# Reordering the last stage of a one-core mixture-of-experts kernel: root chain, last load, stores and last sum

## The reference

```python
x = x + layernorm(attention(layernorm(x)))          # linear attention, 16 heads
x = x + layernorm(ffn(layernorm(x)))
# ffn: out = swiglu(x, shared weights) + sum over the 2 best of 8 experts of w_e * swiglu(x, expert e)
```

## Time and profile before

| what | us |
|---|---|
| three runs | 618.5, 621.85, 625.44 |
| median | 621.85 |
| the profiled execution: device time | 621.5 |
| its span, first to last instruction | 619.8 |
| busy in the span: PE, DVE, ACT, POOL | 456.2, 330.1, 272.4, 270.9 |

### The profile page before, as it was taken

How to read it: one execution, slowest core, us unless ns; L and a number is a source line. 1 busy time by engine, 2 the same in 40 slices (tenths; PEclk the granted TensorE clock), 3 DMA queues, 4 the chain that set the end, 5 groups by cost and what they waited for, 6 DMA issues and landing times.

```text
span 619.8 us, 9478 instructions
## 1 busy us (share of the span) xinstructions
PE 456.2 (74%) x2583; PEld 365.0 (59%) x2592; DVE 330.1 (53%) x1405; ACT 272.4 (44%) x633; POOL 270.9 (44%) x328
## 2 busy tenths in 40 slices
PE   5859888888888983597269963097999987799600
PEld 5637665656565653486258862094689876698600
DVE  6796978787878682155132442032122221795477
ACT  5544655565556551254035620033243544245654
POOL 3000154545454537136745157654026556346620
PEclk9998999999999997599669996589899999799855
DMA  8940010101010103355225442144145557884554
GB/s 254 306 166 2 5 49 32 46 34 45 34 44 34 49 26 125 91 155 158 82 87 158 134 139 66 44 130 153 51 124 167 147 149 221 271 297 147 191 168 192
DMA packets 41622, 73.92 MB, mean 119 GB/s; under 512 B 8803, under 2 KB 23782, under 8 KB 40422
## 3 DMA queue, kind: packets, MB, share of 16 engines
q1 hardware_dynamic: 32870, 54.48, 28.8%
q0 software_dynamic: 8704, 18.89, 8.5%
HBM read 45.82 MB, written 27.53 MB: 118 GB/s over the span
## 4 chain that ended last, share of the span: by engine, by line
PE 43%; DVE 17%; another core or an unknown queue 14%; issue 10%; SPq 6%; ACT 4%; DMA 3%; POOL 2%; DVEq 0%; POOLq 0%; ACTq 0%
PE bank_g L824 6%; PE bank_p L824 6%; PE bank_h L834 6%; PE bank_g L682 3%; PE bank_p L618 3%; PE bank_h L682 3%; PE bank_p L665 3%; DVE st_r L1121 2%; DVE keep L1235 2%; PE bank_t L724 2%; PE bank_g L705 2%; PE bank_t L813 2%; PE bank_t L670 2%; SPq L436 2%
## 5 line engine op out<-in xcount | busy, mean ns | idle before, releaser
L574 POOL DMA_INDIRECT slots_dram<-u_rows,slot_i x128 | 123.8, 967 | 170.5 <-DVE u_rows L1373 106.9
L834 PEld LDWEIGHTS bank_h<-wdn,hid_s 128*128 128x128 f32 x576 | 80.0, 202 | 10.6 <-issue 6.3
L834 PE MATMUL bank_h<-wdn,hid_s 128*128 x576 | 80.7, 285 | 6.7 <-DVE hid_s L1201 3.3
L824 PE MATMUL bank_g<-xbT,wgu_slots 128*128 128x256 f32 x288 | 79.9, 402 | 5.8 <-issue 3.5
L824 PE MATMUL bank_p<-xbT,wgu_slots 128*128 128x256 f32 x288 | 80.1, 404 | 3.6 <-DVE hid_s L1201 2.7
L1201 DVE TENSOR_TENSOR hid_s<-act_s,bank_p 128x512 f32<-128x512 f32 x36 | 24.7, 687 | 91.8 <-ACT act_s L918 42.1
L584 POOL DMA_INDIRECT routed_dram<-pk,yi x40 | 39.1, 976 | 71.6 <-ACT pk L1026 62.4
L1201 DVE TENSOR_TENSOR hid_s<-q_e,bank_p 128x512 f32<-128x512 f32 x36 | 24.6, 683 | 79.0 <-ACT q_e L918 36.7
L824 PEld LDWEIGHTS bank_p<-xbT,wgu_slots 128*128 128x128 f32 x288 | 58.0, 203 | 13.9 <-DVE hid_s L1201 4.0
L824 PEld LDWEIGHTS bank_g<-xbT,wgu_slots 128*128 128x128 f32 x288 | 52.3, 203 | 12.0 <-issue 6.2
L813 PE MATMUL bank_t<-ident,v 128*128 128x128 f32 x72 | 15.6, 299 | 54.6 <-ACT xbT L1012 44.1
(11 more groups left out here) (281 smaller groups left out, 932.9 us busy)
## 6 DMA issues: line engine op xcount, KB each, us to landing
wgu_slots<-wgu_dram SPq DMA_DIRECT2D x72, 256.0 KB
xn<-slots_dram SPq DMA_DIRECT2D x36, 144.0 KB
v<-slots_dram SPq DMA_DIRECT2D x36, 144.0 KB
keep<-in_L_attn_x SPq DMA_DIRECT2D x8, 512.0 KB, 4.0
pair_rows<-routed_dram SPq DMA_DIRECT2D x4, 1024.0 KB
out_dram<-keep SPq DMA_DIRECT2D x8, 512.0 KB, 7.6
wgu_dram<-keep SPq DMA_DIRECT2D x2, 1024.0 KB, 5.3
slots_dram<-u_rows,slot_i POOLq DMA_INDIRECT x128
```

The costliest lines, as they stand in the source:

```text
L574: g.indirect_dma_start(slots_dram, bass.IndirectOffsetOnAxis(ap=slot_i[par][:, c * NT + t:c * NT + t + 1], axis=0), u_row[par][:, t, :], N ...
L824: last = mm(bank[i % 2][:, c * W:(c + 1) * W], w_unit(i)[:, which * INTER + c * P:which * INTER + (c + 1) * P], xbT[:, i % XDEEP, :], star ...
L834: last = mm(bank[:, t * E:(t + 1) * E], hid[:, i % XDEEP, c * W + t * P:c * W + (t + 1) * P], wdn[:, ds(e, 1), c * E:(c + 1) * E].rearrang ...
```

## The change

It does five things, all in the closing stage:

1. Group 3 (batches 5 and 6) has all 8 tiles of a batch scaled by ACT, none by DVE.
2. On DVE the root chain of batches 5 and 6 comes right behind their statistics, with nothing between its instructions. The residual adds of 1 to 4, and then that of 5, come behind it and ahead of the sums of batch 7. The add of 6 stands inside the root chain of 7.
3. The rows of batch 7 are loaded by two DMAs, tokens 0 to 3 and 4 to 7 of each partition, and summed half by half.
4. SP stores batch 0 before it waits for the last scatters. The stores of 1 to 6 come behind a wait until the second half of batch 7's rows has landed.
5. The residual add of batch 7 and its store are made in two halves, tiles 4 to 7 (scaled by DVE) first.

```diff
-C_GROUPS = ((0, 1, 8), (1, 2, 8), (3, 2, 8), (5, 2, 6), (7, 1, 4))
+C_GROUPS = ((0, 1, 8), (1, 2, 8), (3, 2, 8), (5, 2, 8), (7, 1, 4))
 C_HELD = 3
+LAST_HALVES = (1, 0)
...
             for b in range(FIRST, B - 1):
                 load_pair(b)
+            store(0)
             for place in range(YB):
                 for done in y_out[place]:
                     sp.wait_ge(done, 16 * HALF * len(range(place, HALVES, YB)))
-            load_pair(B - 1)
-            for b in range(B):
+            rows, whole = routed_v[B - 1, :, :], pair(B - 1).rearrange("p t c n -> p (t c n)")
+            sp.wait_ge(pair_read, B - SLOTS_C)
+            sp.dma_start(whole[:, 0:NT * E], rows[:, 0:NT * E]).then_inc(pair_in[(B - 1) % SLOTS_C], 16)
+            sp.dma_start(whole[:, NT * E:2 * NT * E], rows[:, NT * E:2 * NT * E]).then_inc(half_in, 16)
+            sp.wait_ge(half_in, 16)
+            for b in range(1, B - 1):
                 store(b)
-            sp.wait_ge(stored, 16 * B)
+            for i, h in enumerate(LAST_HALVES):
+                sp.wait_ge(last_res, i + 1)
+                sp.dma_start(out_v[B - 1, :, h * NT * E // 2:(h + 1) * NT * E // 2], kept(B - 1, h * NT * E // 2, (h + 1) * NT * E // 2)).then_inc(stored, 16)
+            sp.wait_ge(stored, 16 * (B + 1))
...
+            def last_sums():
+
+                g, b = last_g, B - 1
+                for h, loaded in enumerate((pair_in[b % SLOTS_C], half_in)):
+                    part = slice(h * NT // 2, (h + 1) * NT // 2)
+                    dv.wait_ge(loaded, 16 if h else 16 * (b // SLOTS_C + 1))
+                    two = pair(b)[:, part, :, :]
+                    v.tensor_tensor(two[:, :, 0, :], two[:, :, 0, :], two[:, :, 1, :], ALU.add).then_inc(pair_sum, 1)
+                    yield
+                    dv.wait_ge(pair_sum, b + h + 1)
+                    shared = kept(b, (NT + h * NT // 2) * E, (NT + (h + 1) * NT // 2) * E).rearrange("p (t n) -> p t n", n=E)
+                    v.tensor_tensor(shared, shared, two[:, :, 0, :], ALU.add).then_inc(pair_read, 1)
+                    yield
+                    dv.wait_ge(pair_read, b + h + 1)
+                    for t in range(h * NT // 2, (h + 1) * NT // 2):
+                        c_last[g % 2] = inc(v.bn_stats(st_of[g % 2][:, t, :], kept(b, (NT + t) * E, (NT + t + 1) * E)))
+                    yield
+
+            def last_add(h, k):
+
+                z, half = NT * E, NT * E // 2
+                wait(k)
+                v.tensor_tensor(kept(B - 1, h * half, (h + 1) * half), kept(B - 1, h * half, (h + 1) * half), kept(B - 1, z + h * half, z + (h + 1) * half), ALU.add).then_inc(last_res, 1)
...
                 yield True
-                sums = c_sums(C_HELD)
-                for i, _ in enumerate(sums):
-                    yield
+                yield from c_sums(C_HELD)
+                yield from c_scale(C_HELD)
                 for g in range(1, C_HELD):
                     yield from c_add(g, n[0])
-                for g in range(C_HELD, len(C_GROUPS)):
-                    sums = c_sums(g + 1) if g < last_g else iter(())
-                    for _ in c_scale(g):
-                        next(sums, None)
-                        yield
-                    c_norm(g)
-                    normed = n[0]
-                    yield from sums
-                    if g == last_g:
-                        yield from c_add(g - 1, before)
-                    before = normed
-                yield from c_add(last_g, normed)
+                between = c_add(C_HELD, n[0])
+                next(between)
+                yield from last_sums()
+                for i, _ in enumerate(c_scale(last_g)):
+                    if i == 3:
+                        next(between)
+                    yield
+                c_norm(last_g)
+                last_add(LAST_HALVES[0], n[0])
+                dv.wait_ge(y_normed, B)
+                last_add(LAST_HALVES[1], n[0])
+                yield
```

More of the change, by code:

```diff
@@ L324, in program @@
         pair_sum, pair_read = sem("pair_sum"), sem("pair_read")
+        half_in = sem("half_in")
+        last_res = sem("last_res")
         count1 = sem("count1")
```

## The result

The changed kernel ran at a median of 614.9 us (20 runs) against 618.57 for the kernel before (20 runs, among them the three of the table above). The ratio is 0.9927, with a 95% interval of 0.9901 to 0.9954: 4.5 us less, 2.8 to 6.1. The profiled execution took 615.53 us, its span 613.8.

The account below looks back on a forecast made before the run. DVE's queue was taken to bound the end: 19.7 us of work instead of 22.3 wins 2.6, a halved last store 0.8, in all -3.4 us. That gave 618.1, stated as 618.4 us, range 614.8 to 622.0.

Parts of the forecast that it names:

- the anchor: Whole kernel: the profiled execution's forecast of 618.1 us, put 0.35 under the median of 621.85, gave 618.4.
- rival (d): Whole kernel: runs spread over 6.9 us, instruction placement may move the unit stage, anything from 613 to 624; chance 0.12.
- my sum: Closing stage: DVE's work laid out anew from 594.17 takes 19.7 us instead of 22.3; with the last store, -3.4 us.
- the lag: Time from the end of batch 6's statistics to the issue of batch 7's load; 1.9 us in the first profile.
- The signs: Expected profile: no DVE hole above 1 us from 594 to 614, last scatter at 595.9, stage before 594 unmoved.
- The load: Batch 7's rows: halves land at about 600.1 and 602.4 to 602.8; no faster load credited to the stores' absence.
- The covers: Closing stage: ACT, load halves and stores finish ahead of their users, costing 0; the stores have 2.3 us reserve.
- The warning on ACT: DVE's add of batch 5: prediction wrong if ACT has not finished batch 5 by 601.7, since batch 7's sums wait behind.
- The last store: End of kernel: a 256 KB store takes 2.1 us, winning 0.8; bounds 2.1 and 2.9.
- (a): End of the units: the early store's 1.5 us of traffic delays the last scatters, gain 1.9, 619.9 us; chance 0.15.
- (b): Batch 7's load becomes the bound: half two lands at 606.5, DVE waits 1.3 us, 619.7 us; chance 0.12.
- (c): DMA queue ahead of the last halves: stores held together end late, 624.4 us at 200 GB/s; chance 0.04.

Follow-up runs that it names:

- again: The kernel before, run once more unchanged as a scale for the others; ratio 1.0006 to the kernel before.
- after_pair: The changed kernel, run once more unchanged on the same chip and in the same rounds as a further variant; ratio 0.9912 to the kernel before.
- whole_load: The changed kernel with batch 7's rows loaded by one DMA and summed whole instead of in halves; ratio 0.9913 to the kernel before.
- pool_adds: The changed kernel with the residual adds of batches 5 and 6 on GpSimd behind its last scatter; ratio 0.9951 to the kernel before.
- sp_only: The kernel before with batch 0's store early and stores 1 to 7 behind the landing of batch 7's rows, DVE unchanged, one load; ratio 0.9975.
- store0_late: The changed kernel with only batch 0's store put back behind the load of batch 7's rows; ratio 0.9925 to the kernel before.
- dve_only: The kernel before with DVE's new order and batches 5 and 6 scaled on ACT, but one load, whole sums and last add, old SP order; ratio 0.9984.
- lag_before: The kernel before with batch 7's load held back by one more store of batch 0 that SP waits for; ratio 1.0065.
- lag_after: The changed kernel with batch 7's load held back by a second store of batch 0 that SP waits for; ratio 0.9965 to the kernel before.

## Why the prediction was wrong, point by point

**The failing step** is the anchor: "It lies 0.35 under the median, 621.85, so I predict 618.4." Three runs had given that median, two of them among the four highest of the twenty; 20 gave 618.57, 3.3 us less, and again alone moved over 9.6 us (606.4 to 616.0) with not an instruction changed. I had that spread in rival (d) as 0.12 and only 2 us of it in the range, and I took it for something that the change might stir up, not for what the kernel before does by itself. From 618.57 my sum leads to 615.2. The measured 613.3 lies 1.9 below that and 1.5 below the range; the median of all 20 runs, 614.9, is 0.1 inside it. That the three runs lay high was bad luck; to give a median of three a reserve of 2 us was the mistake. Why the same kernel runs at such different levels stays open. The direction was right.

**The size** was 3.4 us, measured 4.5 (2.8 to 6.1), which does not exclude 3.4. The terms of my sum held in the profile: 2.8 + 5.9 + 4.6 + 3.85 + 2.5 = 19.7 us of DVE's work forecast, 19.15 found, each term high by 0.02 to 0.24, the adds most (1.13 us apart, not 1.16 to 1.19). The last add's end to the end of the span became 2.5 instead of 3.3 us, the forecast 0.8. Together 3.9, which after_pair shows at the very lag of before. What the sum lacked is the lag. I took the profile's 1.9 us as the kernel's, and worked out the hole from it. Other executions have 3.2 to 4.9, and there the kernel before ends 1.3 to 3 us later, counted from its statistics, while the new order has slack up to 4.4. At a lag of 3.2 that adds 1.3 us to the gain; at 4.5 and above it is not known in full, since in the profiles with such a lag (again, whole_load, pool_adds) ACT is late as well.

**The signs**: DVE had no hole, and the queues stand in the order forecast. Two signs failed. "The stage before 594" moved, by 2.05 us, and the last load was issued at 595.31, so the last scatter landed at least 0.6 us ahead of the 595.9 forecast. Both are the unit stage, whose place no term of mine covered, and both move more than that between executions of the kernel before.

**The load**: "the stores, issued right behind the load, stood behind it already" was wrong. sp_only shows 4.9 us without them, where before has 6.3 with them. It cost the forecast nothing, since in the new order the load is not waited for, but alone it is 1.4 us in the old order.

**The covers** held: ACT was ahead of the adds, the halves of the load ahead of the sums, the stores of 1 to 6 over before the last halves, the early store free. The warning on ACT was the right one: in whole_load its wait came last.

**The last store**: I took 2.1 us by the rows; 2.02 to 2.09 were measured. By the fixed cost of about 2.0 us that the Trainium skill gives ("DMA: Bandwidth & Descriptors", Anatomy of one DMA, a section on DMAs that GpSimd issues, while SP issues this one) it would have been 2.6; the trace disagrees.

**The rivals**: (a) was not seen, neither in store0_late's ratio nor in its lag (3.2, as with the early store), but its 1.5 us are less than the intervals tell apart, so it is not excluded. (b) fell with after's own waits, (c) with after, in which no packet moved from 610.0 to 611.4; (d) described the level, not the gain.

## What to carry to other kernels

When one engine has a hole while it waits for a transfer, look for its own later work that needs nothing from that transfer, and move the chain that releases another engine to the front: that was some 3.3 of the 5.2 us here at a lag of 3.2. Measure a closing stage from a landmark inside it, and ask of every input (here the lag of the last load) how it varies between executions, because a cut that creates slack can be worth more than one profile shows. Do not take three runs for the level of a kernel whose runs spread over some 10 us. State a time as a ratio to a base that is measured again.

## What the runs showed of the hardware

- A 1 MB load of rows from DRAM took 4.9 us with an empty queue behind it (sp_only, whole_load) and 6.3 to 6.4 with stores queued behind it (before, again, dve_only, lag_before); it lagged before the first packet of a store had moved (88 of its 128 packets against 120, 3.9 us behind the issue). In halves of 512 KB it landed at 4.0 and 5.3 us behind the first issue (lag_after, where the stores begin at 598.62).
- A store of 256 KB landed 2.0 to 2.1 us behind its issue (store0_late, after_pair), one of 512 KB 2.6 to 2.9 with the queue to itself (before, lag_before); one such took 3.8 (lag_after), and why is open.
- GpSimd's add of 128 x 1024 floats took 2.35 to 2.75 us beside DVE, and two of DVE's instructions with two SBUF operands stood still meanwhile (pool_adds); DVE alone needs 1.2 for that add.
- Most of GpSimd's last scatters followed each other every 1.26 to 1.27 us, 0.96 of it busy (before, after).
- The same program, the kernel before, ran at medians of 509 to 618 us in different sets of rounds, at mean granted clocks of 0.95 to 0.96 in the two fast sets and 0.89 to 0.91 in the others, on other chips. The clock differs by 6%, the time by 17%; the rest is open.
